# Local attention in a two-layer decoder kernel: zero products, token sums and the sum over the inverse are taken elsewhere

## The reference, cut to what matters

```python
g = x @ Wg.T + bg;  v = x @ Wv.T + bv               # per head: (b, h, t, 32)
corr = (g @ g.T) / (|g_i| |g_j| + 1e-8)             # cosines
m = (j <= i) & (j >= i - 128)
corr = (corr * m + 1) / 2
denom = mean_j(corr) + 0.5
fitness = 1 / (denom * sum_i(1 / denom))
attn = softmax(where(m, corr * fitness_i, -1e10))
out = (attn @ v) @ Wo.T + bo
```

## Time and profile before

| | us |
|---|---|
| median of 3 runs (2728.8 to 2731.62) | 2728.88 |
| the profiled execution | 2730.75 |
| its span, first to last instruction | 2729.0 |
| TensorE busy in the span | 2614.8 (96%) |
| VectorE busy | 1906.1 (70%) |
| ScalarE busy | 811.5 (30%) |
| GpSimd busy | 868.7 (32%) |

### The profile page before, as it was taken

The page is one execution under the profiler, slowest core; times in us unless marked ns, Lnnn a source line. Parts: engine busy times, 40 slices in busy tenths (PEclk is TensorE's granted clock), DMA queues, the critical chain, the costliest instruction groups (busy, mean ns, idle before and its releaser), DMA issues. The chain is left out here.

```text
span 2729.0 us, 36936 instructions
## 1 busy us (share of the span) xinstructions
PE 2614.8 (96%) x13021; PEld 1581.3 (58%) x13021; DVE 1906.1 (70%) x3326; ACT 811.5 (30%) x1197; POOL 868.7 (32%) x902
## 2 busy tenths in 40 slices
PE   8999998999998889999998879999999999999998
PEld 4444545555555444544444447777777777777775
DVE  4788404666667336666678758888888888888886
ACT  1111322333332246666678611111111111111110
POOL 2232104554554346666678601011111111111000
PEclk9999999999999999999999979999999999999999
DMA  5444130000000133333335511111111111111111
GB/s 172 147 167 149 55 121 1 1 1 1 1 1 1 55 94 95 100 97 95 96 103 148 162 40 41 44 45 45 45 40 43 43 45 42 40 42 45 38 40 37
DMA packets 218915, 175.93 MB, mean 64 GB/s; under 512 B 37839, under 2 KB 184655, under 8 KB 217710
## 3 DMA queue, kind: packets, MB, share of 16 engines
q1 hardware_dynamic: 188054, 148.59, 18.2%
q10 hardware_dynamic: 30680, 24.98, 3.3%
HBM read 90.51 MB, written 52.43 MB: 52 GB/s over the span
## 5 line engine op out<-in xcount | busy, mean ns | idle before, releaser
L2100 PE MATMUL bank<-tiles,tl_XQT 128*128 128x512 f32 (+1 forms) x768 | 327.9, 570 | 0.0
L2105 PE MATMUL bank<-tiles,tl_XQT 128*128 128x512 f32 (+1 forms) x768 | 318.0, 557 | 0.0
L2117 PE MATMUL bank<-tiles,tl_HT 128*128 128x512 f32 x682 | 306.6, 605 | 1.5 <-DMA tl_HT<-tl_tmp 1.5
L2105 PEld LDWEIGHTS bank<-tiles,tl_XQT 128*128 128x128 f32 x768 | 236.7, 308 | 65.6
L2100 PEld LDWEIGHTS bank<-tiles,tl_XQT 128*128 128x128 f32 x768 | 232.3, 310 | 62.4 <-issue 8.9
L2117 PEld LDWEIGHTS bank<-tiles,tl_HT 128*128 128x128 f32 x682 | 218.1, 324 | 74.0 <-issue 8.9
L1404 POOL TENSOR_SCALAR_AFFINE_SELECT tiles<-tiles 128x512 f32<-128x512 f32 x256 | 181.5, 711 | 186.4 <-ACT tiles L1644 171.2
L2052 POOL TENSOR_TENSOR tl_rs<-tl_ve,mhalf 128x1 f32<-128x1 f32 x29 | 16.0, 551 | 549.9 <-DVE tl_ve L2252 549.9
L2176 ACT ACTIVATE tl_HQ<-bank 128x512 f32<-128x512 f32 (+1 forms) x96 | 54.0, 562 | 411.0 <-PE bank L2100 381.9
L1751 DVE SCALAR_TENSOR_TENSOR tiles<-tiles,bank 128x1024 f32<-128x1024 f32 (+1 forms) x128 | 141.7, 1148 | 20.0 <-PE bank L1512 19.9
L1409 POOL TENSOR_SCALAR_AFFINE_SELECT tiles<-tiles 128x512 f32<-128x512 f32 x224 | 154.5, 690 | 0.0
(11 more groups left out here) (307 smaller groups left out, 4998.4 us busy)
## 6 DMA issues: line engine op xcount, KB each, us to landing
tl_HT<-tl_tmp SPq DMA_DIRECT2D x248, 44.0 KB, 1.9
tl_HT<-tl_tmp ACTq DMA_DIRECT2D x248, 44.0 KB, 2.0
fp_weights<-space_quant ACTq DMA_DIRECT2D x33, 256.0 KB, 2.1
X<-in_x SPq DMA_DIRECT2D x8, 1024.0 KB, 10.4
v<-tiles SPq DMA_DIRECT2D x32, 256.0 KB, 2.4
unit_g<-tiles SPq DMA_DIRECT2D x32, 256.0 KB, 2.4
unit_gT<-tiles SPq DMA_DIRECT2D x32, 256.0 KB, 2.8
la_GN<-unit_g SPq DMA_DIRECT2D x128, 64.0 KB, 2.0
```

What stands on the lines that cost most here:

```text
L2100: mm = e.matmul(bank[(2 * q) % 3][:, 0:w], chunk(XQT[n % 2], c), WgT[q][:, :, c, :], start=(c == 0), stop=(c == C - 1))
L2105: mm = e.matmul(bank[(2 * q + 1) % 3][:, 0:w], chunk(XQT[n % 2], c), WuT[q][:, :, c, :], start=(c == 0), stop=(c == C - 1))
L2117: mm = e.matmul(bank[DOWN][:, :], chunk(HT, q), WdT[:, q, :], start=(q == 0), stop=(q == IC - 1))
```

## The change

Three things. First, `start_bank` and its two constant tiles are gone: the first product into a bank carries the start flag, and the products behind it in that bank do not. A product that would fall half on columns already written and half on fresh ones is split in two (the gathers of the second and third tile of each half), or ordered behind the one that writes first (the last tile of the half before; the values of the odd tile before). Second, ScalarE copies the transposed unit vectors in four pieces of 128 columns and writes out the sum of each piece, which is a tile's sum over tokens; VectorE's `tile_sums` is replaced by `pair_sums`, two small operations a batch entry. Third, the second product of `inverse` writes out its own sum, and the reduce behind it is gone. Waits on `s_pv` count fewer steps, through `used`. The diff, without the declarations of semaphores:

```diff
--- before.py
+++ after.py
...
-        ones16 = sb("ones16", [P, DH], BF16)
-        empty = sb("empty", [P, D], BF16)
-        gsum, gpair = sb("gsum", [P, G]), sb("gpair", [P, G])
+        gsum, gpair = sb("gsum", [P, NC * G]), sb("gpair", [P, NC * G])
...
@@ -1237,6 +1235,8 @@
         there = lambda n: 0 <= n < NS
         tile = lambda m: 0 <= m < NT
         s_next = sem("next_stage_weights")
+
+        used = lambda y: s_pv.at((y + 1) // 2 + 1 if y >= 0 else 0)
         ROUNDS = range(-AHEAD - 4 * BEFORE - 4, NS + LAG + 2, 2)
 
         projected = lambda p: (p // 4 + BEFORE, p // 2 % 2)
@@ -1301,7 +1301,7 @@
                     for n, last in enumerate(LAST_IN):
                         x = NS - RING + last
                         if s == (x + 3) // 2 * 2:
-                            e.wait_ge(s_pv.sem, s_pv.at(x + 1))
+                            e.wait_ge(s_pv.sem, used(x))
                             c, w = PIECES[n]
                             for r, at in enumerate((GATE_AT[n], UP_AT[n])):
                                 e.dma_start(k.tiles[:, at:at + C * w].rearrange("p (i d) -> p i d", d=D),
@@ -1363,7 +1363,7 @@
                         if there(x):
                             y = x - TILES
                             if y % 2:
-                                e.wait_ge(s_pv.sem, s_pv.at(y + 2))
+                                e.wait_ge(s_pv.sem, used(y))
                             else:
                                 e.wait_ge(s_pair.sem, s_pair.at(y // 2 + 1))
                             load_tile(VN, d_vn, k.VNd, x)
@@ -1382,8 +1382,6 @@
 
                 e.memset(LR[:, :], 1.0).then_inc(s_zero.sem, 1)
                 e.memset(RR[:, :, :], 0.0).then_inc(s_zero.sem, 1)
-                e.memset(ones16[:, :], 1.0).then_inc(s_begin.sem, 1)
-                e.memset(empty[:, :], 0.0).then_inc(s_begin.sem, 1)
 
                 e.memset(MC[:, :], 1.0).then_inc(s_mc.sem, 1)
                 e.wait_ge(s_mc.sem, s_mc.at(1))
@@ -1467,31 +1465,27 @@
                                       start=True, stop=True)
                     mm.then_inc(s_arg.sem, 1)
 
-                def start_bank(n):
-                    for h in range(HC):
-                        mm = e.matmul(bank[n][DH * h:DH * h + DH, :], ones16[:, :], empty[:, :], start=True, stop=False)
-                    return mm
-
                 def gather(p):
                     n, t = p // G, p % G
                     if t == 0:
                         e.wait_ge(s_z.sem, s_z.at(2 * n))
-                        start_bank(WB)
                     if t == HG:
 
                         e.wait_ge(s_z.sem, s_z.at(2 * n + 1))
-                        start_bank(WB)
-                        for h in range(HC):
-                            q = slice(DH * h, DH * h + DH)
-                            e.matmul(bank[WB][q, 0:P], GN[(p - 1) % TILES][:, q], TR[(p - 1) % RING][:, h, P:WIN],
-                                     start=False, stop=False)
                     e.wait_ge(d_gn[p % TILES].sem, d_gn[p % TILES].at(16 * (p // TILES + 1)))
                     e.wait_ge(s_TM.sem, s_TM.at(p + 1))
                     c, w = (t % HG) * P, P if t % HG == HG - 1 else WIN
-                    for h in range(HC):
-                        q = slice(DH * h, DH * h + DH)
-                        mm = e.matmul(bank[WB][q, c:c + w], GN[p % TILES][:, q], TR[p % RING][:, h, 0:w],
-                                      start=False, stop=(t % HG == HG - 1))
+
+                    for j0, j1 in ((0, P), (P, w)) if t % HG in (1, 2) else ((0, w),):
+                        for h in range(HC):
+                            q = slice(DH * h, DH * h + DH)
+                            mm = e.matmul(bank[WB][q, c + j0:c + j1], GN[p % TILES][:, q], TR[p % RING][:, h, j0:j1],
+                                          start=(t % HG == 0), stop=(t % HG == HG - 1))
+                    if t == HG:
+                        for h in range(HC):
+                            q = slice(DH * h, DH * h + DH)
+                            mm = e.matmul(bank[WB][q, 0:P], GN[(p - 1) % TILES][:, q], TR[(p - 1) % RING][:, h, P:WIN],
+                                          start=False, stop=False)
                     mm.then_inc(s_gat.sem, 1)
 
                 def dots(x):
@@ -1514,13 +1508,13 @@
                                       start=True, stop=True)
                     mm.then_inc(s_d.sem, 1)
 
-                def values(x, j0, w, last=False):
+                def values(x, j0, w, first=False, last=False):
 
                     t = x % G
                     c = ((t + j0 // P) % 2) * P
                     for h in range(HC):
                         q = slice(DH * h, DH * h + DH)
-                        e.matmul(bank[PVS][q, c:c + w], VN[x % TILES][:, q], TR[x % RING][:, h, j0:j0 + w], start=False, stop=False)
+                        mm = e.matmul(bank[PVS][q, c:c + w], VN[x % TILES][:, q], TR[x % RING][:, h, j0:j0 + w], start=first, stop=False)
                     for h in range(HC):
                         q = slice(DH * h, DH * h + DH)
                         mm = e.matmul(bank[PVS][q, WIN + c:WIN + c + w], k.ones[:, 0:DH], TR[x % RING][:, h, j0:j0 + w],
@@ -1531,17 +1525,16 @@
                     n, t = x // G, x % G
                     if t % 2 == 0:
                         e.wait_ge(s_ao.sem, s_ao.at(x // 2))
-                        mm = start_bank(PVS)
-                        if t == 0 and x:
-                            mm.then_inc(s_pv.sem, 1)
-                        if t:
-                            values(x - 1, P, P).then_inc(s_pv.sem, 1)
                     e.wait_ge(d_vn[x % TILES].sem, d_vn[x % TILES].at(16 * (x // TILES + 1)))
                     e.wait_ge(s_pm.sem, s_pm.at(x + 1))
                     if t % 2 == 0:
-                        values(x, 0, WIN).then_inc(s_pv.sem, 1)
+
+                        mm = values(x, 0, WIN, first=True)
+                        if t:
+                            mm = values(x - 1, P, P)
+                        mm.then_inc(s_pv.sem, 1)
                     else:
-                        values(x, 0, P, True).then_inc(s_pair.sem, 1)
+                        values(x, 0, P, last=True).then_inc(s_pair.sem, 1)
 
                 def sums(n, r, p):
                     e.wait_ge(s_z.sem, s_z.at(2 * n + r + 1))
@@ -1640,7 +1633,7 @@
                 def tanh(p):
                     t = p % G
                     e.wait_ge(s_arg.sem, s_arg.at(p + 1))
-                    e.wait_ge(s_pv.sem, s_pv.at(p - RING + 1))
+                    e.wait_ge(s_pv.sem, used(p - RING))
                     e.activation(TR[p % RING][:, :, 0:cols(t)], four(ARG[:, :])[:, :, 0:cols(t)], ACT.Tanh).then_inc(s_T.sem, 1)
 
                 def exp(x):
@@ -1685,7 +1678,10 @@
                 def unit_transposed(m):
                     e.wait_ge(s_gt.sem, s_gt.at(m + 1))
                     e.wait_ge(d_gq[m % 2].sem, d_gq[m % 2].at(16 * (m // 2)))
-                    e.activation(GQ[m % 2], bank[3][:, :], ACT.Copy).then_inc(s_gc.sem, 1)
+                    for c in range(C):
+                        x, at = slice(c * P, (c + 1) * P), (m // G * C + c) * G + m % G
+                        i = e.activation(GQ[m % 2][:, x], bank[3][:, x], ACT.Copy, accum_out=gsum[:, at:at + 1])
+                    i.then_inc(s_gc.sem, 1)
 
                 def v_scaled(m):
                     e.wait_ge(s_v.sem, s_v.at(m + 1))
@@ -1750,25 +1746,20 @@
                     e.wait_ge(s_d.sem, s_d.at(x - x % 2 + 2))
                     e.scalar_tensor_tensor(out=y, in0=y, scalar=1.0, in1=d, op0=ALU.add, op1=ALU.mult).then_inc(s_u.sem, 1)
 
-                def tile_sums(n, h):
-                    tiles = slice(HG * h, HG * h + HG)
+                def pair_sums(b):
+                    at = lambda v: v[:, b * C * G:(b + 1) * C * G].rearrange("p (c t) -> p c t", c=C)
+                    e.wait_ge(s_gc.sem, s_gc.at(G * (b + 1)))
+                    e.tensor_copy(at(gpair)[:, :, 0:1], at(gsum)[:, :, 0:1]).then_inc(s_gp.sem, 1)
+                    e.tensor_tensor(at(gpair)[:, :, 1:G], at(gsum)[:, :, 0:G - 1], at(gsum)[:, :, 1:G], ALU.add).then_inc(s_gp.sem, 1)
+
+                def z(n, h):
+                    e.wait_ge(s_gp.sem, s_gp.at(2 * (n // C) + 2))
                     e.wait_ge(d_gt[n % 2][h].sem, d_gt[n % 2][h].at(16 * (n // 2 + 1)))
-                    e.tensor_reduce(gsum[:, tiles], GT[n % 2][:, h * D:(h + 1) * D].rearrange("p (t q) -> p t q", t=HG), AX.X,
-                                    ALU.add).then_inc(s_gs.sem, 1)
-                    e.wait_ge(s_gs.sem, s_gs.at(2 * n + h + 1))
-                    if h == 0:
-                        e.tensor_copy(gpair[:, 0:1], gsum[:, 0:1]).then_inc(s_gp.sem, 1)
-                        e.tensor_tensor(gpair[:, 1:HG], gsum[:, 0:HG - 1], gsum[:, 1:HG], ALU.add).then_inc(s_gp.sem, 1)
-                    else:
```

(25 more changed lines are left out.)

## The result

The changed kernel takes 2740.22 us (median of 6 runs, 2738.84 to 2742.32) against 2730.05 us for the kernel before in the same comparison: ratio 1.0037, 95% interval [1.0027, 1.0048], 10.2 us slower. Forecast were 2742.0, a range of 2722 to 2756 and "slower" with a chance of 0.66. The profiled execution has a span of 2738.2 us (before 2729.0).

What follows compares the result with a forecast made beforehand. TensorE, 96% busy, bounds 1042 to 1412 us; afterwards a chain through several engines does. Terms -8.1 - 0.9 + 0.8 + 23.7 - 2.9 = +12.6 us on the median give 2741.5, said as 2742, range 2722 to 2756.

Steps and rivals of the forecast that it cites:

- the cost of the sums: ScalarE's four copies with sums, ahead of the next round's dots: 23 x 1.03 = 23.7 us lost.
- the 0.5 that would have spoken against it: Sign of a wrong forecast: dots starting within 0.5 us of their present distance from the transposes.
- The wait that ends last at that place: Dots' wait for ScalarE's copy of transposed unit vectors: delaying the copy delays TensorE by the same amount; 7.2 us before.
- D: How much longer ScalarE's four copies with sums last than the one copy: taken as 1.03 us, bounds 0.18 to 1.58.
- cheap sums: Rival at ScalarE's copies: reads of some 0.1 us each, D 0.24 to 0.72, no change, about 2729; chance 0.20.
- My own case: At ScalarE's copies: D between 0.72 and 1.4, making the kernel 5.5 to 21.1 us slower; chance 0.50.
- The lower bound without sums: ScalarE's four copies, overlapping by 0.11 us each and sums free, last 0.77 us, D = 0.18.
- The zeros: TensorE's zero products removed and gathers split: 8.1 and 0.9 us gained, 0.8 lost.
- The 22 groups: Zero groups opening the gathering bank before 1412 us, covered by late arguments' wait for ScalarE: booked at nothing.
- the 38: Zero groups opening the values' bank in TensorE's unbroken work: two give nothing, 36 x 0.225 = 8.1 us gained.
- The inverse sum: VectorE's reduce over the inverse replaced by an accumulated sum, ahead of waiting dots: 0.57 us, five times, 2.9 us gained.
- sums free: Rival at ScalarE's copies: sums hide in the copy, D = 0.18, 2722 us; break-even D = 0.48; chance 0.14.

Runs made afterwards that it cites:

- zeros and inverse sum: Against the kernel before: zero products gone, gathers split, inverse's product writes its own sum; ScalarE's copy and VectorE's token sums as before. 2728.19 us, ratio 0.9991.
- sums one round behind: Changed kernel, but unit vectors copied by one instruction, and ScalarE sums the copied tile in the next round. 2727.16 us, 0.9987 against the kernel before.
- zeros only: Against the kernel before: zero products gone and gathers split; copies, token sums and the inverse's sum as before. 2726.4 us, ratio 0.9985.

## Why the prediction was right, and where it was not

The direction and the mechanism were right. That the number is only 2 us off is luck: the cost of the sums was booked 9 us too high and the gain of the rest 7 us too high, and the two offset each other. Of the signs that it named, the wait of the dots for the copies was 16.9 us and not 28, the short ScalarE instructions last 1.13 us and not 1.6, and the dots start 0.53 us further from the transposes than before, just beyond the 0.5 that would have spoken against it.

- **The place.** "The wait that ends last at that place": confirmed. D shows up whole in the wait for the copies, 9.7 us over 18 waits, and again where I said a tanh would carry it: the arguments' wait for the tanh is 13.8 and was 12.2 in the kernel of zeros and inverse sum, 1.6 = 3 x 0.54 more. Three waits of dots for line 1701, a copy that ScalarE makes right behind, grew from 2.1 to 3.7 against the same kernel, by another 1.6. Together 12.9 us in 24 places; moving the sums one round behind gave 13 back. I had counted 23, since my view ended at 1420 us: the last copy of the kernel before starts at 1421.6 and has dots behind it too, and eight, not nine, lie before 990.
- **From wait to time.** Not all of D reached the time. Over the projections 17 of these waits grew by 9.2 us, and the stretch got 7.8 longer than with zeros and inverse sum; four copies between two dots in the middle (1160.32 to 1238.39, against 1153.84 to 1230.06) cost 1.85 us and not 2.16, 0.46 each. I had carried D over whole.
- **The size of D: the step that failed.** I took 1.03, in the middle between two ways of overlapping; the trace says 0.54. I had a read cost 0.267 and wait for its copy's last element. It takes 0.22, and starts 0.16 us into a copy of 0.28. This puts D into what I called "cheap sums" (0.24 to 0.72), to which I gave 0.20 together with other causes. Term: 24 x 0.54 = 13.0 instead of 23.7. My own case (0.72 to 1.4, chance 0.50) did not come; its outcome did. The lower bound without sums, 0.77 us for four pieces, was right: 0.78. The Trainium skill's figures (ScalarE: Activation LUTs, What ACT_TABLE_LOAD costs) gave 0.89 us for the same, 0.11 too much here.
- **The zeros.** Booked -8.1 - 0.9 + 0.8 = -8.2; measured -3.9. The 22 groups at nothing were right: without them the arguments wait for ScalarE instead, 3.4 us more. Of the 38, I checked only the round behind a table load for a later wait. The round with late arguments has one in every chunk, for the tanh, and the next round one for the scores, so a chunk gained 0.5 and not 0.82: over 335 us, with one chunk each 38.6, 4.3 us. Ahead of the first dots there was no gain but a loss: 1.7 us in the kernel of zeros only, all of it one stretch in which four products took 5.40 us. The late stretch and what follows gave 0.8 of the 0.9 booked.
- **The inverse sum.** Booked -2.9; measured nothing (+0.8, interval -1.6 to +3.3). The wait went, as said (5.9 to 0.7). The step that failed here is that I never asked what is late next. It was GpSimd's mask, 0.93 us at the gathers, and the scores. That the accumulated sum is an instruction of its own, as the Trainium skill says (VectorE: DVE Perf Modes, Two Vector instructions with no wait between them), the trace confirms: 76 to 86 ns on VectorE, inside my bounds of nothing and 0.15.
- **The clock.** Not in my sum: in the changed kernel the arguments waited 3.07 us for a tanh (2.53 before), and the four products behind them took 6.52 us where they took 5.05. With 5.40 instead of 3.70 twice more (1033.94 and 1560.09) that is 4.9 us in this one execution. The windows view has 992 to 1042 us at a granted clock of 0.90, before 0.97: more of it at the lower level of 1.2 GHz. The windows row and the timeline of the changed kernel:

```profile
992.00:1042.00 50.00, 40.39 (x239) 18.98 (x242) 14.20 (x36) 24.10 (x52) 23.84 (x26) 0.90 0.31 87
...
994.35 0.61 PE L1464 MATMUL bank<-la_RR,la_LR 32*128 32x512 bf16 x2 [3.07 <-ACT tiles L1637]
994.88 6.52 PE L1555 MATMUL bank<-home_T,tiles 128*128 128x512 f32 x8
...
1004.28 3.70 PE L1567 MATMUL bank<-home_odd,tiles 128*128 128x512 f32 x8
...
1033.94 5.40 PE L1567 MATMUL bank<-home_odd,tiles 128*128 128x512 f32 x8
```

With the clock the account closes. From entry to the next stage the changed kernel took 681.7 us and that of zeros and inverse sum 667.3: 14.4 more. The clock has 3.2 of it (6.52 for 5.07, and 5.40 for 3.70 at 1560.09; the 5.40 near 1032 us is in both), which leaves 11.2 for the delayed copies: 0.47 for each of 24 places, as in the middle of the stage. The sum by measured terms is -3.9 + 11.2 + 3.2 + 0 = +10.5, against 10.2 measured. The clock's part is that of one execution, and no run separates it from the waits that it came with; the sums priced by whole kernels, 13.1 and 14.5, include it. It also follows that the rival "sums free" had its break-even wrong. With 3.9 us on the other side it lies at D = 3.9/24 = 0.16, below what merely cutting the copy in four costs.

## What to carry to other kernels

An accumulated sum on ScalarE is cheap in work (0.09 us of pace behind a copy here), and costs nearly its full length (0.46 of 0.54 us here) if it is put ahead of the release of a bank that TensorE waits for: release the bank with one copy, and take the sum from the copied tile in a gap of the engine. Before booking work removed from an engine that is 96% busy as gained, look at every round of a period for the wait that comes next; more than a third of the gain booked in each chunk (0.82 us, of which 0.5 came) lay where another engine would have been waited for. And a wait that goes is worth nothing until the next one at that place is named.

## What was not expected of the hardware

A read of ScalarE's accumulator overlaps the copy that it reads out: start to start 0.16 us, with copies of 272 to 297 ns and reads of 204 to 232 ns, 92 of each from 990 to 1420 us. From SBUF, in the kernel with the sums one round behind, a copy and its read took 0.29 us from start to start instead of 0.25 from PSUM. And less work on TensorE near the start of the stage came with a lower granted clock there: 0.97 before, 0.93 without the zeros, 0.90 with the longer waits as well. Work without a result put back there brought 0.97 again, once with a lower clock just ahead of it instead, and no time that the traces credit to it.
